# A three-layer block with a state-space scan: scan steps, their decays and the sums over states spread evenly over the units, three scan steps moved behind the next unit's first sums of squares

## What is computed

```python
x = x + 0.5 * ffn(layernorm(x), A, B, W, bias)
x = x + scan(layernorm(x), W_xproj, W_dt, b_dt, A_log, D_param)
x = x + 0.5 * ffn(layernorm(x), A, B, W, bias)

# ffn
vecs = einsum('arh,bsh->bsar', A, x)             # 64 experts x 16
_, idx = top_k(norm(vecs, axis=-1), 4)
routes = one_hot(idx, 64).sum(-2) / 4
v = einsum('bsa,bsar->bsr', routes, vecs)
return x @ W.T + bias + einsum('bsa,ajr,bsr->bsj', routes, B, v)

# scan: 1024 channels x 16 states, 2048 steps in time
delta = softplus(delta_r @ W_dt.T + b_dt)
h = exp(delta * A) * h + delta * B_t * x_t
y = sum(h * C_t, axis=-1)
return y + x * D_param
```

## Time and profile before

| what | value |
| --- | --- |
| median of 3 runs (lowest to highest) | 2836.99 us (2836.76 to 2839.64) |
| the profiled execution | 2846.45 us |
| its span, first to last instruction | 2844.7 us |
| busy shares of the span | PE 92%, POOL 83%, DVE 78%, ACT 53% |
| mean granted TensorE clock | 0.98 |
| longest kinds of work | POOL's products with B and C, DVE's scans (1280.2 us), PE's f16 matmuls |

### The profile page before, as it was taken

The page is one execution under the profiler, slowest core; times in us unless marked ns, Lnnn a source line. Parts: engine busy times, 40 slices in busy tenths (PEclk is TensorE's granted clock), DMA queues, the critical chain, the costliest instruction groups (busy, mean ns, idle before and its releaser), DMA issues.

```text
span 2844.7 us, 39804 instructions
## 1 busy us (share of the span) xinstructions
PE 2612.2 (92%) x13597; PEld 1183.5 (42%) x13664; DVE 2218.2 (78%) x2933; ACT 1499.8 (53%) x3363; POOL 2349.2 (83%) x703
## 2 busy tenths in 40 slices
PE   4989999999999999898999989999999998888999
PEld 1444444444344444343444434444444433444444
DVE  8447878878888788787878878788788887887843
ACT  5355656565555554555555545555455454555521
POOL 2038988999999998899999989999899998988920
PEclk8999999999999999999999999999999999999999
DMA  5144444544454444544453445544454444453321
GB/s 217 55 113 131 138 126 130 158 147 129 135 143 133 145 122 140 133 135 139 135 162 114 136 134 155 152 125 126 140 157 143 135 127 125 137 138 126 99 63 52
DMA packets 303520, 373.50 MB, mean 131 GB/s; under 512 B 148435, under 2 KB 220243, under 8 KB 303318
## 3 DMA queue, kind: packets, MB, share of 16 engines
q1 hardware_dynamic: 286422, 337.40, 40.2%
q10 hardware_dynamic: 16896, 33.56, 4.0%
HBM read 234.05 MB, written 103.29 MB: 119 GB/s over the span
## 4 chain that ended last, share of the span: by engine, by line
PE 35%; DVE 33%; ACT 8%; DMA 8%; DVEq 7%; issue 5%; POOL 2%; ACTq 1%; SPq 1%; POOLq 0%
DVE mreg L1136 18%; PE pv L544 12%; PE po L544 7%; PE pv L548 6%; PE po L548 4%; ACT pA L922 3%; DMA delta_scratch<-mreg 3%; DMA mreg<-xnT_scratch 2%; PE py L710 2%; DVE pv L1097 2%; DVEq L1052 2%; PE pv L673 2%; DVE sel L1105 2%; DVE sel L1094 2%; DVEq L1102 2%
## 5 line engine op out<-in xcount | busy, mean ns | idle before, releaser
L512 POOL TENSOR_TENSOR mreg<-mreg 128x2048 f32<-128x2048 f32 x256 | 1161.6, 4538 | 70.8 <-ACT hst L908 70.6
L1136 DVE TENSOR_TENSOR_SCAN mreg<-pA,hst,mreg 128x512 f32<-128x512 f32 (+1 forms) x1024 | 1038.6, 1065 | 77.9 <-ACT hst L908 58.1
L922 ACT ACTIVATE pA<-mreg,nA 128x512 f32<-128x512 f32 (+1 forms) x1280 | 742.4, 596 | 458.6 <-DVE mreg L1136 415.9
L502 POOL TENSOR_TENSOR mreg<-mreg 128x1024 f32<-128x1024 f32 x340 | 795.8, 2365 | 223.4 <-DMA mreg<-delta_scratch 209.9
L544 PE MATMUL pv<-wA,xT 128*128 128x512 f16 x2016 | 471.9, 389 | 59.9 <-ACT xT L829 49.0
L544 PE MATMUL po<-wB,uT 128*128 128x512 f16 x2016 | 472.1, 383 | 15.6 <-DVE xin L1060 10.9
L544 PE MATMUL po<-wW,xT 128*128 128x512 f16 x2016 | 467.4, 380 | 6.5 <-issue 4.5
L496 POOL TENSOR_TENSOR mreg<-mreg 128x2048 f32<-128x2048 f32 x86 | 390.2, 4537 | 20.8 <-issue 20.8
L544 PEld LDWEIGHTS pv<-wA,xT 128*128 128x128 f16 x2016 | 196.0, 100 | 343.3 <-ACT xT L829 96.1
L1078 DVE TENSOR_REDUCE n<-sel 128x32 f32<-128x512 f32 x128 | 87.0, 680 | 306.5 <-ACT sel L837 306.4
L544 PEld LDWEIGHTS po<-wB,uT 128*128 128x128 f16 x2016 | 191.3, 98 | 293.5 <-issue 71.7
(11 more groups left out here) (132 smaller groups left out, 2376.4 us busy)
## 6 DMA issues: line engine op xcount, KB each, us to landing
mreg<-delta_scratch SPq DMA_DIRECT2D x256, 512.0 KB, 6.0
delta_scratch<-mreg ACTq DMA_DIRECT2D x128, 256.0 KB
xin<-x SPq DMA_DIRECT2D x32, 512.0 KB, 5.2
x_scratch<-xin SPq DMA_DIRECT2D x32, 512.0 KB, 3.9
xnT_scratch<-auxs SPq DMA_DIRECT2D x32, 512.0 KB, 2.9
mreg<-xnT_scratch SPq DMA_DIRECT2D x64, 256.0 KB, 7.0
yT_scratch<-mreg SPq DMA_DIRECT2D x64, 256.0 KB, 2.3
uT<-yT_scratch SPq DMA_DIRECT2D x32, 512.0 KB, 4.6
```

Source lines behind the costliest of these rows:

```text
L502: pool.tensor_tensor(h[:, half * n:half * n + n, :], u, b.broadcast_to([P, n, c.width]), ALU.mult).then_inc(s_bm, 1)
L512: pool.tensor_tensor(h, h, by_c, ALU.mult).then_inc(s_cm, 1)
L922: last = nc.scalar.activation(dst[:, part, :], src[:, part, :], ACT.Exp, scale=nA[:, m:m + 1])
L1136: last = V.tensor_tensor_scan(h, split(pA[:, i % 2, :], c)[:, part, :], h, before, ALU.mult, ALU.add)
```

## The change

1. **Blocks.** A unit of SCAN0 to SCAN1 no longer has whole groups, but 1024/57 blocks: 18 of them in all units but two (17). `block_at(a, twentieths)` says how many of them are due at each of the 20 positions, so `scans(5, 7)`, for one, issues one block, where it issued two. `decays` follows two blocks ahead as before. `sum_up` of tile t stands before block 16t + 24, as it did, but now wherever in a unit that block falls.
2. **Sums over states.** `states(a, third)` has 18 places in a unit of PE, one after each third of `base`, `routed` and `experts`. Group G is due with block 4G + 10. What would fall on the places 12 and 13, inside the first half of `experts`, goes to 11, ahead of it. Of the 256 sums 42 stand at 14, 15 and 16, behind the next unit's first half of `experts` and ahead of the end of its second: one each in the units 4 to 31 and in 33, 35, ... 59.
3. **DVE's order.** Positions 17 to 19, three blocks, are issued after `sums(b, 0)`; positions 18 and 19 stood ahead of it.
4. SP, POOL and the positions of a tile's delta are as they were.

```diff
+    for a in us[SCAN0:SCAN1]:
+        a.block0 = (a.u - SCAN0) * 4 * NGRP // (SCAN1 - SCAN0)
+        a.block1 = (a.u + 1 - SCAN0) * 4 * NGRP // (SCAN1 - SCAN0)
+    us[SCAN1].block0, us[SCAN1].block1 = 4 * NGRP, 4 * NSL
...
+    for G in range(NGRP):
+        due = 4 * G + 10
+        a = next(a for a in us[SCAN0:] if due < a.block1)
+        third = (due - a.block0) * 18 // (a.block1 - a.block0) - 1
+        a.sums[11 if third in (12, 13) else max(third, 0)].append(G)
...
+        def block_at(a, twentieths):
+
+            return a.block0 + (twentieths * (a.block1 - a.block0) + 10) // 20
...
                 def decays(lo, hi):
 
-                    for i in range(lo, hi):
-                        if count and i < count + 2:
-                            decay(first + i)
+                    if SCAN0 <= a.u < SCAN1:
+                        for i in range(block_at(a, lo - 2), block_at(a, hi - 2)):
+                            decay(i + 2)
...
                 def scans(lo, hi):
-                    for i in range(lo, hi):
-                        if i % 4 == 0:
-                            sum_up(a, i // 4)
-                        if i < count:
-                            scan(first + i)
+                    for i in range(block_at(a, lo), block_at(a, hi)):
+                        if i % 16 == 8 and i >= 24:
+                            sum_up(i // 16 - 1)
+                        if i < 4 * NGRP:
+                            scan(i)
...
-                scans(15, 18)
+                scans(15, 17)
                 result(a, 1)
                 delta(a, 2)
                 if a.kind == 1:
                     dve.drain()
                     dve.wait_ge(s_xn2, a.w)
                     stats("ln2", xin[:, a.p, :], s_mv2)
-                scans(18, 20)
                 if b:
                     sums(b, 0)
+                scans(17, 20)
...
-                if b:
-                    experts(b, 0, 0)
...
-                states(a, 4)
+                for nb in range(2):
+                    for third in range(3):
+                        if b:
+                            if (nb, third) == (1, 0):
+                                pe.wait_ge(s_dc, a.z_end)
+                            experts(b, nb, third)
+                        states(a, 12 + 3 * nb + third)
```

More of the change, by code:

```diff
@@ L26, in __init__ @@
         self.slots = []
+        self.block0, self.block1 = 0, 0
+        self.sums = [[] for _ in range(18)]
         self.zs = {}
@@ L283, in slot_of @@
             return a.slots[n] if n < len(a.slots) else None
-        def blocks_in(a):
-            groups = [g for g in a.slots if g < NGRP]
-            return (4 * groups[0], 4 * len(groups)) if groups else (0, 0)
+        def block_at(a, twentieths):
+            return a.block0 + (twentieths * (a.block1 - a.block0) + 10) // 20
         @block.sync
@@ L694, in z, with states, sum_states @@
                 last.then_inc(s_z, 1)
[L696 to L701, removed]
+            def states(a, third):
+                for G in a.sums[third]:
+                    sum_states(G)
+            def sum_states(G):
                 g = G % 4
@@ L718, in unit @@
                 base(a, 0, 0)
+                states(a, 0)
                 if late:
@@ L721, in unit @@
                 base(a, 0, 1)
-                states(a, 0)
+                states(a, 1)
                 base(a, 0, 2)
@@ L726, in unit @@
                 z(a, 0)
+                states(a, 2)
                 base(a, 1, 0)
@@ L733, in unit @@
                     y_blocks(y, 1)
+                states(a, 3)
                 base(a, 1, 1)
+                states(a, 4)
                 base(a, 1, 2)
-                states(a, 1)
+                states(a, 5)
                 if late:
@@ L745, in unit @@
                     turn_products(late)
+                states(a, 6)
                 routed(a, 0, 1)
@@ L748, in unit @@
                     pe.wait_ge(s_pc, late.w + 1)
+                states(a, 7)
                 routed(a, 0, 2)
-                states(a, 2)
+                states(a, 8)
                 routed(a, 1, 0)
                 z(a, 1)
+                states(a, 9)
                 routed(a, 1, 1)
@@ L757, in unit @@
                     norm_blocks(b, 1)
+                states(a, 10)
                 routed(a, 1, 2)
-                states(a, 3)
+                states(a, 11)
                 z(a, 2)
-                if b:
-                    experts(b, 0, 0)
[L763 to L773, removed]
-                states(a, 4)
+                for nb in range(2):
[5 more added lines that the diff above has]
+                        states(a, 12 + 3 * nb + third)
             norm_blocks(US[0], 0)
@@ L1137, in scan, with sum_up @@
                 last.then_inc(s_sc, 1)
-            def sum_up(a, n):
-                S = slot_of(a, n)
-                if S is None or S < 6 or (S - 6) % 4:
-                    return
-                t = (S - 6) // 4
+            def sum_up(t):
                 dve.wait_ge(s_e, 4 * t + 4)
```

2 lines of the change are left out of this document (removed).

## The result

The changed kernel takes 2873.3 us (median of 4 runs, 2866.0 to 2876.12), the kernel before beside it 2838.31 us (2836.76 to 2844.38): a ratio of 1.0115, 95% interval 1.0098 to 1.0133. By the ratio it is slower by 33 us (the medians differ by 35), where 7 us less was forecast, and it lies 11 us above the range.

What follows compares the result with a forecast made beforehand. PE alone bounds units without scans; with scans a DVE, ACT and PE loop mostly ends last, a little behind PE. Terms -15 + 18 - 5 - 5 = -7 us on 2846.45 give about 2839.5, or 2830 against the median; range 2792 to 2862.

Steps and rivals of the forecast that it cites:

- 56 scans -68: DVE ahead of the statistics, units 4 to 59: one scan fewer per unit, 1.21 us each where the chain ends last.
- loads -5: `add_y` waits for tokens in units 24, 32, 40 and 56: 4 x -1.2 = -5 us, bounds 0 and -9.4.
- 42 inner +45: Sums over states on PE between the first squares and the end of `experts`: +1.07 us each where the chain ends last.
- waits -5: PE's sums that wait for POOL's product or `sum_up`: new spacing takes 5 of 15.5 us off.
- late squares +63 and +3: Second squares on ACT late: +63 us behind 29 units of kind 1, +3 behind six of kind 2.
- late before -35: Credit for second squares already late behind 14 five-group units of kind 1: 14 x 2.5 = 35 us.
- hidden -5: Eight units (33, 35, ... 47) where PE nearly ended last: half of a scan's time hidden, estimated at -5 us.
- It comes off the chain in every unit: The scan saved at `scans(5, 7)` on DVE: -1.21 us where the chain ends last, nothing where PE does.
- One behind `sum_up`: Sums over states on PE would stand one block behind `sum_up`, part of taking 5 us off their waits.
- the slower one: Rival: lateness of the second squares on ACT comes through in full, 2857 us; slower by 6 to 45 us, chance 0.33.
- Its condition: Slower rival decides if kind 1's second squares are over 2 us late against PE where an inner sum should hide part.
- Its sign: Sign of the slower rival: units of kind 2 that follow kind 1 become longer than 44.5 us.

Runs made afterwards that it cites:

- e10: Kernel before with the even spread of scans and decays alone, sums over states at the five old places, DVE's old order: 2800.84 us, ratio 0.9864.
- e2: Changed kernel with DVE's order of before, its last scans ahead of the next unit's first sums of squares again: 2815.4 us, ratio 0.9902.
- e9: Kernel before with only DVE's new order, positions 17 to 19 behind the next unit's first sums of squares: 2877.31 us, ratio 1.0136.
- e11: Kernel before with only two ACT edits, `normed2` and the next unit's second squares ahead of decays: 2848.73 us, ratio 1.0029.
- e3: Changed kernel with `normed2` ahead of the decay at position 19 on ACT: 2836.49 us, ratio 0.9986.
- e4: Changed kernel with the next unit's second squares ahead of the last two decays on ACT: 2829.27 us, ratio 0.9959.
- e5: Changed kernel with both ACT edits, `normed2` ahead of its decay and the second squares ahead of the last two decays: 2798.44 us, ratio 0.9851.
- e7: Changed kernel with both ACT edits of e5 and DVE's order of before: 2828.45 us, ratio 0.9945.
- e14: Changed kernel with softplus of a tile at position 0 one decay earlier on ACT: 2863.26 us, ratio 1.0083.
- e1: Changed kernel with the 42 sums over states inside the chain put behind the whole of `experts`: 2865.21 us, ratio 1.0079.
- e13: e5 with the 42 inner sums over states put behind `experts`, other new places kept: 2779.56 us, ratio 0.9788.
- e16: e13 with softplus of a tile at position 0 one decay earlier on ACT: 2776.11 us, ratio 0.9778.

## Why the prediction was wrong

The sum had three parts in it that the runs now price one by one, by their ratios: the blocks from before to e10, the places of the sums from e10 to e2, DVE's order from e2 to the changed kernel.

| part | in the sum, us | measured, us | change of the gap, us |
| --- | --- | --- | --- |
| even blocks: 56 scans -68, loads -5 | -73 | -39 | +14 |
| places of sums: 42 inner +45, waits -5 | +40 | +11 | -26 |
| order: late squares +63 and +3, late before -35, hidden -5 | +26 | +60 | +57 |
| together | -7 | +33 | +45 |

The last column is needed because the three parts are not independent: the first two edits moved lateness too, and the -35 of the third row was meant against the kernel before, while e2 has only 19 us of late squares left. Where only an order was changed, the gap and the time went together:

| only an order differs | change of the gap, us | change of the time, us |
| --- | --- | --- |
| before to e9 (DVE's) | +39 | +39 |
| before to e11 (ACT's) | +8 | +8 |
| e2 to the changed kernel (DVE's) | +57 | +60 |
| changed kernel to e3 (ACT's) | -37 | -37 |
| changed kernel to e4 (ACT's) | -43 | -44 |
| changed kernel to e5 (ACT's) | -69 | -75 |
| e5 to e7 (DVE's) | +23 | +27 |

- **The late squares were seen, and in the unit that I had worked out their size was right** (8.0 us from squares to squares, 2.9 late; the row has 8.00 and 2.9). The step that failed is their net price, the third row: +26 us, where the lateness grew by 45 us and, by the table, each us of it cost about one. Three things in it were off. The gross was 66 us and measured 76: behind kind 1 the squares are late by 2.4 us on average, not 2.2, and behind kind 2 by 7 us in all, not 3. The credit "less what was late before" was 14 x 2.5 = 35 us, for a lateness that measures 31. And nothing shows the 5 us that were to be hidden.
- **What the old lateness had cost stays open.** No run took it away alone. The table says what an added us costs, not what the first ones did. A unit behind it can have given back no more than PE idled in it; counted so, unit by unit, there is room for some 22 of the 31 us. In the units 16, 18 and 26 PE idles for only 0.92, 0.29 and 0.61 us, less than the 2.1, 1.2 and 2.5 us that the squares ahead of them were late. So the credit was too large by 4 us, and perhaps by 13.
- **With these the sum comes close.** Scans -68, inner sums +45, late squares +76, late before -31 (or -22), the softplus wait of the next point +10, `add_y`'s waits -6 (9.4 to 3.2 us) make +26 (or +35); measured +33. This sum was made after the runs.
- **"It comes off the chain in every unit" failed in the units with a tile's delta at position 0.** The scan at `scans(5, 7)` stood in front of DVE's `delta`, which now waits for softplus, 19.0 us in 16 units. I had asked what is late next for the squares, but not for this scan. e14 shows that 9 to 10 us of it mattered.
- **The places of the sums were priced about right for this kernel.** The sum had +45 for the 42 inner ones and gave 21 of it back as lateness hidden behind kind 1 and 10 behind kind 2, 14 net. e1 has some 43, 34 given back, and 8 to 10 net. In a kernel without lateness 1.07 us each would be too much: it is 0.45 there (e5 to e13).
- **"One behind `sum_up`" was no margin.** Behind a late unit DVE's `sum_up` is late as well, and a tile's first sum on PE waits for it: 16.4 us in place of 7.2, up to 4.19 in unit 39. The sum took 5 us off for the waits of sums. The prediction named the mask and the copies as queued behind the squares and left `sum_up` and `gather` out. In e5, with no lateness, the wait for `sum_up` is back at 7.2 us, so it is one of the ways in which lateness reaches PE and not a price on top of it.

PE, unit 39 of the changed kernel:

```profile
1823.41 1.93 PE L721 MATMUL py<-mreg,Em 128*32 128x512 f32 x8 [4.19 <-DVE mreg L1157]
```

- **Behind units of kind 2 the sum held.** The prediction's terms give some 5 us of gain for the fourth stretch (12 x -1.21, inner sums +6, the six behind a unit without one +3); it has 5.5. There is some luck in this: the six are late by 6 us together, twice the +3.
- **The rival that came about is the slower one**, at 2857 us, 16 too low. Its mechanism held in the main: the lateness came through. Its condition, over 2 us of lateness where an inner sum should hide a part, held in 9 of these 20 units; most of the others have 1.8, as the forecast had it. It was given 0.33, next to 0.30 for the forecast itself, and the range ended at 2862. Its sign named the wrong units: those of kind 2 behind kind 1 are 43.1 us long on average, from mask to mask, and were 42.9, not over 44.5; the late mask lengthens the unit of kind 1 that ends with it.
- That PE's own work is last without scans stands: 103.76 us for units 60 to 62. But its 91% of busy time hid 97 us that e16 got out (2873.3 - 2776.1), partly from the busy time itself, as the last section shows. The Trainium skill ("Perfetto Trace Analysis", section "Identifying the Most-Contended Engine") says that matmul busy time tells little of how near TensorE is to its limit; the runs agree for the stretches with scans. It names two measures to go by instead, the FLOP rate and the share of weight loads; the second told these kernels not apart: 41% in the changed kernel, 42% before.

## What to carry to other kernels

When work is moved into an engine's idle gap, follow the inputs it needs: the scans fitted into DVE's gap, but their decays came to stand in front of the work on ACT that ends the gap. Two engines' orders that feed each other have to be changed together, and a mixture can be worse than both: with even blocks, old and old take 2815 us (e2), new and new 2798 (e5), but new on DVE alone 2873 (the changed kernel) and new on ACT alone 2828 (e7). Lateness is best added up over all units, before and after, on each engine that it can move to; here a us more of it cost about a us. Whether a us less would have given one back in the kernel before was not tried, so a credit for old lateness needs the idle time of the engine that waits behind it as its bound.

The best version found is e16, or e13 within the measurement: 2776 to 2780 us, 2.1 to 2.2% below the kernel before. It has the even blocks and the new order on DVE, `normed2` and the squares ahead of the decays on ACT, and no sum over states inside `experts`.

## What was not expected of the hardware

That PE's busy time would fall. The prediction said that PE's total stays, and put the granted clock at nothing. For the clock that held in the step to the changed kernel: it is 0.980 in both profiled executions. It did not hold for the faster versions. The granted clock and the page of e2, then of e16, with the same 13597 records of matmuls as the changed kernel's 2622.7 us:

```profile
core 0: 2812.4 us, clock 0.987
PE 2597.2 (92%) x13597; PEld 1175.6 (42%) x13664; DVE 2221.3 (79%) x2933; ACT 1497.8 (53%) x3363; POOL 2349.0 (84%) x703
...
core 0: 2774.3 us, clock 0.989
PE 2583.9 (93%) x13597; PEld 1175.2 (42%) x13664; DVE 2225.3 (80%) x2933; ACT 1494.0 (54%) x3363; POOL 2347.9 (85%) x703
```

Of the 61.9 us between the spans of the changed kernel and e2, 25.5 are busy time of PE; of the 100 us to e16 it is 38.8. The rest is idle time. So a part of what less waiting gave came as faster matmuls, and the us for us in the table above contains it. No run holds the clock fixed, so how much of the busy time is due to it alone is not shown.

The timeline shows such places. One is unit 39, whose sum is shown above; stretches of the changed kernel around it, in the columns of the earlier trace rows:

```profile
1815.00:1819.00 4.00, 4.00 (x22) 1.99 (x20) 3.91 (x4) 2.31 (x6) 4.00 (x3) 1.00 0.07 27
...
1823.41:1825.34 1.93, 1.93 (x9) 0.27 (x10) 1.93 (x2) 0.69 (x1) 1.22 (x1) 0.50 0.90 183
```

The granted clock was 1.00 ahead of the 4.19 us wait and 0.50, the lower of the two levels (1.2 GHz), while the eight matmuls ran, in 1.93 us where they take 1.06 to 1.07 at the higher one. The wait cost 0.9 us more than itself there. Another is unit 36, where PE waited 3.74 us for the low part and the clock is 0.50 from 1717.20 to 1720.50 us.
